# Placing edges in block-pair order: eight-tile groups that overlap, with counts made two groups ahead

## The reference, cut to what matters

```
h = relu(layernorm(x)); x = x + gated_conv(h, edge_attr, src, dst)   # z=[h[src],h[dst],e]; sigmoid(bn(zW1))*softplus(bn(zW2)), summed by dst
h = relu(layernorm(x)); x = x + sage(h, src, dst)                     # mean of h[src] by dst
h = relu(layernorm(x)); x = x + masked_hops(h, src, dst)              # three times: edge mask by a small MLP, then a sum by src
h = relu(layernorm(x)); x = x + edge_mlp(h, edge_attr, src, dst)      # mean over dst of MLP([h[src], e])
```

## Time and profile before

| what | value |
|---|---|
| time, median of three executions | 14558.93 us |
| the profiled execution: first to last instruction (span) | 14378.1 us |
| time outside the span (median less span) | 180.8 us |
| stage_place, from about 200 us to about 3440 us of the span | 3240 us |
| DVE busy over the whole span | 8318.0 us (58%) |
| PE busy over the whole span | 9017.0 us (63%) |
| POOL busy over the whole span | 4344.6 us (30%) |

### The profile page before, as it was taken

How to read it: one execution, slowest core, us unless ns; L and a number is a source line. 1 busy time by engine, 2 the same in 40 slices (tenths; PEclk the granted TensorE clock), 3 DMA queues, 4 the chain that set the end, 5 groups by cost and what they waited for, 6 DMA issues and landing times. The chain is left out here.

```text
span 14378.1 us, 449799 instructions
## 1 busy us (share of the span) xinstructions
PE 9017.0 (63%) x157729; PEld 8352.6 (58%) x157730; DVE 8318.0 (58%) x17981; ACT 6707.3 (47%) x18063; POOL 4344.6 (30%) x4481
## 2 busy tenths in 40 slices
PE   6444444444886555897777656666556765566776
PEld 6444444444886544887666556666556665566665
DVE  5333333334888999998163494552954619636146
ACT  0111111112897555896612425985248862389420
POOL 2444444443332000111151241431423414224044
PEclk9997555555998887998867868658676586775875
DMA  4222222101998776996974878869788697787886
GB/s 158 74 74 71 76 74 68 22 17 49 346 346 272 201 202 175 306 323 201 336 249 148 310 247 286 281 204 327 246 270 295 200 336 246 252 312 234 329 305 198
DMA packets 1161871, 3115.28 MB, mean 217 GB/s; under 512 B 367968, under 2 KB 652642, under 8 KB 1150562
## 3 DMA queue, kind: packets, MB, share of 16 engines
q1 hardware_dynamic: 899278, 2289.91, 45.4%
q0 software_dynamic: 262144, 823.09, 19.7%
q10 hardware_dynamic: 276, 0.01, 0.0%
HBM read 1917.81 MB, written 1128.54 MB: 212 GB/s over the span
## 5 line engine op out<-in xcount | busy, mean ns | idle before, releaser
L502 POOL DMA_INDIRECT rows_s<-place_rec,place_index x1568 | 1525.2, 973 | 1892.7 <-DVEq L623 1223.8
L2029 ACT ACTIVATE hop_parts<-hop_x,mask 128x64 f32<-128x64 f32 x6048 | 1524.3, 334 | 11.4 <-issue 7.0
L513 ACT COPY place_oh_turned<-place_turn_ps 100x1024 bf16<-100x1024 bf16 x197 | 199.4, 1012 | 2846.9 <-remote 2017.4
L1876 POOL DMA_INDIRECT mask_cols<-cols_all,mask_index x864 | 841.9, 974 | 2110.2 <-ACT mask_index L1883 1915.9
L2069 PE MATMUL hop_sums_ps<-hop_parts,hop_onehot 128*128 128x64 bf16 x18144 | 1123.9, 241 | 457.6 <-DVE hop_parts L2048 360.9
L2069 PEld LDWEIGHTS hop_sums_ps<-hop_parts,hop_onehot 128*128 128x128 bf16 x18144 | 988.5, 130 | 595.3 <-issue 594.9
L2013 POOL DMA_INDIRECT hop_x<-cols_all,hop_index x864 | 822.6, 952 | 1655.8 <-ACT hop_index L2020 988.0
L538 PE MATMUL place_same_ps<-place_oh_turned 100*128 100x128 bf16 x1568 | 197.5, 306 | 1652.5 <-ACT place_ohd_turned L514 1154.2
L2045 DVE TENSOR_TENSOR hop_parts<-hop_parts 128x448 f32<-128x448 f32 x864 | 540.4, 625 | 1198.4 <-ACT hop_parts L2029 1037.8
L538 PEld LDWEIGHTS place_same_ps<-place_oh_turned 100*128 100x128 bf16 x1568 | 151.3, 138 | 1670.5 <-issue 1670.5
L1959 DVE TENSOR_TENSOR mask_hidden<-mask_part_ps,mask_cols 128x448 f32<-128x448 f32 x864 | 534.4, 619 | 890.4 <-DMA mask_cols<-cols_all,mask_index 567.8
(11 more groups left out here) (382 smaller groups left out, 27979.1 us busy)
## 6 DMA issues: line engine op xcount, KB each, us to landing
cols_all<-att_in_rows SPq DMA_DIRECT2D x216, 896.0 KB
mask_onehot<-hot_s SPq DMA_DIRECT2D x216, 896.0 KB
cols_all<-hop_in_rows SPq DMA_DIRECT2D x216, 896.0 KB
hop_onehot<-hot_s SPq DMA_DIRECT2D x216, 896.0 KB
rows_all<-blank SPq DMA_DIRECT2D x72, 1808.0 KB
ct_u<-rows_all SPq DMA_DIRECT2D x288, 452.0 KB
cm_v<-rows_all SPq DMA_DIRECT2D x288, 448.0 KB, 3.7
cm_onehot<-hot_d POOLq DMA_DIRECT2D x288, 448.0 KB
```

Of the source, the lines that this page charges most:

```text
L502: nc.gpsimd.indirect_dma_start(m.rows_s.rearrange("p n w -> (p n) w"), bass.IndirectOffsetOnAxis(index[:, j, t:t + 1], 0), rec[:, j, t, :] ...
L1876: nc.gpsimd.indirect_dma_start(cols[:, s * 4 + i, :], None, table, bass.IndirectOffsetOnAxis(index[:, s * 4 + i, :], 0)).then_inc(arrived[ ...
L2029: last = nc.scalar.activation(parts[:, i, 0, t * F:(t + 1) * F], x[:, s * 4 + i, t, :], ACT.Copy, scale=mask[:, bass.ds(it * BATCH + t, 1)])
```

## The change

The diff touches `stage_place` and the size of `m.blk` (padding of 24 in place of 8 columns, since one-hots are now made three groups ahead). `turn_ps`, `run_ps` and `runs` get two buffers, `oh` four. The column `run_ps[:, 0, :]`, written once with zeros, makes the base counts of all eight tiles and the new total one operation (`start_runs`), and the total is kept in `runs[:, b, G, :]` in place of `m.run`. ACT signals `turned` after each of its two copies. PE's `find` is split into `compare` and `find`. PE's order becomes `count(g + 2)`, `compare(g + 1)`, `find(g + 1)`, in a loop over four groups per round, and DVE's `step(g)` makes the base counts of group g + 1, ranks group g, picks, makes the one-hots of group g + 3, and sums up. POOL's and SP's programs are unchanged.

```diff
--- before.py
+++ after.py
@@ -382,7 +382,7 @@
             @block.vector
             def _(dve):
                 o = Order(dve, order)
-                o.mark(nc.vector.memset(m.blk[:, EC:EC + 8, :], -1.0))
+                o.mark(nc.vector.memset(m.blk[:, EC:EC + 24, :], -1.0))
@@ -455,18 +455,19 @@
             return ctx.enter_context(nc.sbuf_tensor(f"place_{n}", s, d))
         rec = sb("rec", [P, 2, 16, RW])
         index = sb("index", [P, 2, 16], i32)
-        oh = sb("oh", [P, 2, G, 2, NBK], bf16)
+        oh = sb("oh", [P, 4, G, 2, NBK], bf16)
         oh_turned = sb("oh_turned", [2 * NBK, 2, G, P], bf16)
         ohd_turned = sb("ohd_turned", [NBK, 2, G, P])
-        runs = sb("runs", [NBK, G, 2 * NBK])
+        runs = sb("runs", [NBK, 2, G + 1, 2 * NBK])
         same = sb("same", [P, G, P], bf16)
         rank, slot = sb("rank", [P, 16]), sb("slot", [P, 16, 2])
         picked_v = sb("picked_v", [P, G, 2, NBK])
         ints = [sb(f"int{i}", [P, 16], i32) for i in range(8)]
         seventh = sb("seventh", [P, 16])
         we_parts = sb("we_parts", [P, 3, 3 * F], bf16)
-        turn_ps = ctx.enter_context(nc.psum_tensor("place_turn_ps", [P, G, P], bf16))
-        run_ps = ctx.enter_context(nc.psum_tensor("place_run_ps", [P, G + 1, NBK], fp32))
+        turn_ps = [ctx.enter_context(nc.psum_tensor(f"place_turn_ps{j}", [P, G, P], bf16)) for j in range(2)]
+        run_ps = [ctx.enter_context(nc.psum_tensor(f"place_run_ps{j}", [P, 512], fp32))[0:NBK, 0:(G + 1) * NBK]
+                  .rearrange("p (t n) -> p t n", n=NBK) for j in range(2)]
         same_ps = ctx.enter_context(nc.psum_tensor("place_same_ps", [P, G, P], fp32))
         slot_ps = ctx.enter_context(nc.psum_tensor("place_slot_ps", [P, G, P], fp32))
         e_came = [sem(f"e_came{j}") for j in range(2)]
@@ -507,48 +508,64 @@
 
             @block.scalar
             def _(act):
-                def turn_out(g, h):
+                def turn_out(g, b):
                     act.wait_ge(counted, g + 1)
+                    act.wait_ge(found, g)
                     act.sem_inc(gate, 1)
-                    nc.scalar.copy(oh_turned[:, h, :, :], turn_ps[0:2 * NBK, :, :])
-                    nc.scalar.copy(ohd_turned[:, h, :, :], turn_ps[0:NBK, :, :]).then_inc(turned, 1)
-                turn_out(0, 0)
+                    nc.scalar.copy(oh_turned[:, b, :, :], turn_ps[b][0:2 * NBK, :, :]).then_inc(turned, 1)
+                    nc.scalar.copy(ohd_turned[:, b, :, :], turn_ps[b][0:NBK, :, :]).then_inc(turned, 1)
+                act.sem_inc(found, 1)
+                act.wait_ge(counted, 1)
+                nc.scalar.copy(oh_turned[:, 0, :, :], turn_ps[0][0:2 * NBK, :, :]).then_inc(turned, 1)
+                nc.scalar.copy(ohd_turned[:, 0, :, :], turn_ps[0][0:NBK, :, :]).then_inc(turned, 1)
+                turn_out(1, 1)
                 with act.Fori(0, GROUPS // 2) as k:
                     for h in range(2):
-                        act.wait_ge(found, k * 2 + h + 1)
-                        turn_out(k * 2 + h + 1, 1 - h)
+                        turn_out(k * 2 + h + 2, h)
 
             @block.tensor
             def _(pe):
-                def count(g, h):
+                def count(g, h, b):
                     pe.wait_ge(hot, g + 1)
+                    pe.sem_inc(gate, 1)
                     for t in range(G):
-                        nc.tensor.transpose(turn_ps[0:2 * NBK, t, :], oh[:, h, t, :, :].rearrange("p i n -> p (i n)"), m.ident_b[:])
+                        nc.tensor.transpose(turn_ps[b][0:2 * NBK, t, :], oh[:, h, t, :, :].rearrange("p i n -> p (i n)"), m.ident_b[:])
                     for upto in range(1, G + 1):
                         for t in range(upto):
-                            last = nc.tensor.matmul(run_ps[0:NBK, upto, :], oh[:, h, t, 0, :], oh[:, h, t, 1, :],
+                            last = nc.tensor.matmul(run_ps[b][:, upto, :], oh[:, h, t, 0, :], oh[:, h, t, 1, :],
                                                     start=t == 0, stop=t == upto - 1)
                     last.then_inc(counted, 1)
 
-                def find(g, h):
-                    pe.wait_ge(turned, g + 1)
+                def compare(g, b):
+                    pe.wait_ge(turned, g * 2 + 1)
                     pe.wait_ge(ranked, g + 1)
                     pe.sem_inc(gate, 1)
                     for t in range(G):
-                        last = nc.tensor.matmul(same_ps[:, t, :], oh_turned[:, h, t, :], oh_turned[:, h, t, :], start=True, stop=True)
+                        last = nc.tensor.matmul(same_ps[:, t, :], oh_turned[:, b, t, :], oh_turned[:, b, t, :], start=True, stop=True)
                     last.then_inc(same_done, 1)
+
+                def find(g, b):
+                    pe.wait_ge(turned, g * 2 + 2)
                     pe.wait_ge(ran, g + 1)
                     pe.wait_ge(picked, g + 1)
                     pe.sem_inc(gate, 1)
                     for t in range(G):
-                        last = nc.tensor.matmul(slot_ps[:, t, 0:2 * NBK], ohd_turned[:, h, t, :], runs[:, t, :], start=True, stop=True)
+                        last = nc.tensor.matmul(slot_ps[:, t, 0:2 * NBK], ohd_turned[:, b, t, :], runs[:, b, t, :], start=True, stop=True)
                     last.then_inc(found, 1)
-                count(0, 0)
-                with pe.Fori(0, GROUPS // 2) as k:
-                    for h in range(2):
-                        find(k * 2 + h, h)
-                        pe.wait_ge(turned, k * 2 + h + 1)
-                        count(k * 2 + h + 1, 1 - h)
+                for j in range(2):
+                    nc.tensor.matmul(run_ps[j][:, 0, :], m.zeros_b[:, 0:NBK], m.zeros_b[:, 0:NBK], start=True, stop=True)
+                count(0, 0, 0)
+                count(1, 1, 1)
+                compare(0, 0)
+                find(0, 0)
+                with pe.Fori(0, GROUPS // 4) as k:
+                    for i in range(4):
+                        g = k * 4 + i
+                        pe.wait_ge(turned, g * 2 + 2)
+                        pe.wait_ge(ran, g + 1)
+                        count(g + 2, (i + 2) % 4, i % 2)
+                        compare(g + 1, (i + 1) % 2)
+                        find(g + 1, (i + 1) % 2)
 
             @block.vector
             def _(dve):
@@ -556,45 +573,51 @@
                 dve.sem_inc(ranked, 1)
                 dve.sem_inc(picked, 1)
                 o.mark(nc.vector.memset(rec[:, :, :, EF + 3:RW], 0.0))
-                for t in range(G):
-                    o.mark(nc.vector.tensor_copy(runs[:, t, NBK:2 * NBK], m.shift_d[:]))
+                for b in range(2):
+                    o.mark(nc.vector.tensor_copy(runs[:, b, 0:G, NBK:2 * NBK], b2(m.shift_d[:], G)))
 
                 def hots(at, h):
                     nc.vector.tensor_tensor(oh[:, h, :, :, :].rearrange("p t i n -> p (t i) n"), b2(m.numbers[:], 2 * G),
                                             b3(m.blk[:, at, :].rearrange("p t i -> p (t i)"), NBK), ALU.is_equal).then_inc(hot, 1)
 
-                def rank_group(g, h, s):
-                    dve.wait_ge(counted, g + 1)
+                def start_runs(b, before):
+                    nc.vector.tensor_tensor(runs[:, b, :, 0:NBK], run_ps[b][:, 0:G + 1, :], b2(before, G + 1), ALU.add).then_inc(ran, 1)
+
+                def step(g, i, s):
+                    half = i % 2
+                    dve.wait_ge(counted, g + 2)
+                    dve.wait_ge(found, g + 1)
+                    dve.wait_ge(ran, g + 1)
                     dve.sem_inc(gate, 1)
-                    s.mark(nc.vector.tensor_copy(runs[:, 0, 0:NBK], m.run[:]))
-                    s.then(nc.vector.tensor_tensor(runs[:, 1:G, 0:NBK], run_ps[0:NBK, 1:G, :], b2(m.run[:], G - 1), ALU.add))
-                    dve.sem_inc(gate, 1)
-                    nc.vector.tensor_tensor(m.run[:], m.run[:], run_ps[0:NBK, G, :], ALU.add).then_inc(ran, 1)
-                    hots(bass.ds(g * G + G, G), 1 - h)
+                    start_runs((i + 1) % 2, runs[:, half, G, 0:NBK])
                     dve.wait_ge(same_done, g + 1)
                     dve.sem_inc(gate, 1)
                     for t in range(G):
                         last = nc.vector.scalar_tensor_tensor(out=same[:, t, :], in0=same_ps[:, t, :], scalar=2.0, in1=m.after[:],
                                                               op0=ALU.is_equal, op1=ALU.mult,
-                                                              accum_out=rank[:, h * G + t:h * G + t + 1])
+                                                              accum_out=rank[:, half * G + t:half * G + t + 1])
                     last.then_inc(ranked, 1)
-                    dve.wait_ge(found, g + 1)
-                    dve.wait_ge(ran, g + 1)
+                    dve.wait_ge(found, g + 2)
+                    s.wait()
                     dve.sem_inc(gate, 1)
                     nc.vector.tensor_tensor(picked_v[:], slot_ps[:, :, 0:2 * NBK].rearrange("p t (i n) -> p t i n", i=2),
```

(14 more changed lines are left out.)

4 lines of the change are left out of this document (2 added, 2 removed).

## The result

On the chip that ran both, the kernel before took 14562.22 us (14557.95 to 14574.15) and the changed kernel **14138.85 us** (14123.64 to 14160.53), four runs each: ratio 0.971, interval 0.9698 to 0.9722. That is 423 us less. The forecast was 540 less and 14,019 us; it has the sign and most of the size, and the time lies in the range.

A forecast was written before the change was run, and what follows sets the result against it. The placing stage was taken as a chain of waits, 33.06 us a pair. Held signal at 20.3 plus 7.2 us gives 27.5, saving 545 us over 98 pairs; with +5 once, 14558.93 - 540 = 14,019 us, range 13,340 to 14,440.

The forecast's parts named there:

- The hold: In the placing stage, PE's signal from inside a POOL DMA burst arrives late: 12.9 us a pair, 95 times in 98.
- The end of the hold: Late signal comes 20.3 us after the burst begins (7.4 + 12.9), as before the change; at most +22.8 us.
- rival B: PE itself is held, so compare and find follow the hold: 31.4 us a pair, 14,400 us; chance 0.10.
- rival A: No hold left, POOL bounds the stage: 20.9 to 21.3 us a pair, 13,370 to 13,410 us; chance 0.25.
- The sentence on what would make it wrong altogether: Wrong if the hold grew with PE's instructions in a burst, or if time outside the stage moved; no size given.
- Main case: All the hold stays, 7.2 us of work follows: 27.5 us a pair, 14,019 us; DVE waits at picking; chance 0.47.
- second variant: The coming group's count is held at +5.8 us; DVE waits at base counts, 9.0 us follows in place of 6.2.
- Base counts: One DVE addition on 50x450, 0.61 us, replaces three operations: saves 0.28 us a group, 0.56 a pair.
- One-hots later: DVE's one-hots move behind the picking, ahead of `placed` for the second group: +0.99 us on that chain.
- C: The hold comes once per round of PE's loop: 24.2 us a pair on the mean, 13,690 us; chance 0.04.
- D: Slower: hold catches PE inside the count ahead of compare and find, 33.9 to 36.7 us a pair; chance 0.07.
- F: PE's longer loop body stalls on instruction fetch, 12.9 us in each of 49 rounds: 14,650 us; chance 0.02.

The follow-up runs named there:

- e3: Changed kernel with only the first of each pair's 16 indirect DMAs, stage alone read: 13.62 us a pair.
- e4: Changed kernel with a 512-column POOL memset (0.54 us) as a pause behind each indirect DMA: 13882.27 us, ratio to before 0.9662.
- e7: Kernel before with a 512-column POOL memset (0.54 us) as a pause behind each indirect DMA: 13838.67 us, ratio to before 0.9531.
- e9: Changed kernel with 8 count matmuls a group in place of 36 and a 304-column pause (0.37 us) behind each DMA: 13607.44 us, ratio to before 0.948.
- e10: Kernel before with 8 count matmuls a group in place of 36 and a 304-column pause (0.37 us) behind each DMA: 13542.19 us, ratio to before 0.9433.
- e12: Kernel before with only the first of each pair's 16 indirect DMAs, stage alone read: 19.56 us a pair.
- e2: Kernel before with 8 count matmuls a group in place of 36, nothing else: 13968.8 us, ratio to before 0.9719.
- e8: Kernel before with base counts and new total by one addition in place of a copy and two additions: 14341.88 us, ratio to before 0.9874.
- e11: Changed kernel with each DMA row writing 16 bytes in place of 144, to another table, stage alone read: 29.33 us a pair against 30.24.
- e1: Changed kernel with 8 count matmuls a group in place of 36: 13897.44 us, ratio to before 0.9671.
- e5: Changed kernel with 8 count matmuls a group in place of 36 and a pause giving DMAs 1.40 us apart: 13809.25 us, ratio to before 0.9504.

## Why the prediction was right, and where it was not

*The stage and the order of reading.* Right: the stage is a chain of waits, the rest is constant to 25 us, no more than other traces differ in it, and the gain is that of the waits that the new order takes out. The forecast of 540 us was 117 too high.

*The hold.* Half right. "PE's signal from inside a burst arrives late" is what happens: 97 late counts before, 55 after, none in the six kernels without a back-to-back burst (e3, e4, e7, e9, e10, e12). But the text made it a fixed delay that ends 20.3 us after the burst begins and leaves PE itself alone. Two terms failed:

- *The end of the hold.* Put at +20.3 (range to +22.8). In after the late signals come at +24.8 us (median), 4.8 us behind the end of POOL's last DMA. Before, the median is +21.4, and 46 of the 97 come while POOL is still writing, so they aren't tied to the burst's end.
- *PE's rate.* "PE has made the first group's find and the count after it" by +4.7 us, "at about +7.5 us PE ends L544 of the second group": PE's busy time of 15.0 us a pair was laid under the burst at full speed. From +12 us of a first burst to the end of the second PE begins 1 to 3 instructions per us, so the rest of the chain goes one instruction at a time until POOL stops. That is rival B's mechanism ("PE itself is held"), which was put at 0.10 because the matmuls 0.7 us apart in the earlier trace rows had been seen once.

*The sum.* 27.5 us a pair was forecast and 30.24 is in the trace; the ratio gives 423 / 98 = 4.3 us a pair gained against 5.56. It isn't one pair of 30 but a short one of 21 (rival A's value) and a long one of 38 to 41: counts two groups ahead let one burst start on the heels of the other, and then 32 DMAs pass with PE at a crawl. A steady 27.5 was wrong in kind, and that it is near the mean of 21 and 39.5 is partly luck. The base it was taken from was off as well: 33.06 is a trace of before with a span of 14378.1 us, and beside after before took 14,562.

*The sentence on what would make it wrong altogether.* Its first half came true: the loss grows with PE's instructions in a burst. e2 shows it: 28 matmuls and their loads less a group, 2.8% off the old order with no wait moved. The gain stood nevertheless, because the new order removes 5.9 us a pair of its own (19.56 to 13.62 without bursts), of which 4.3 are left with them.

*Where DVE's long wait is.* Main case: at the picking; second variant: at the base counts. It is at the base counts (L584, 1421.8 us, 45 waits; L603 has 67.8 us). So it is the count of the coming group that is held, for which the text had 9.0 us of tail: 20.3 + 9.0 = 29.3 us a pair, against 30.24. The choice of 7.2 between 6.2 and 9.0 is one step of the overestimate.

*Base counts.* One addition on 50x450 at 614 ns, forecast 0.61. The saving of 0.56 us a pair was right as DVE's time and too small for what e8 gained, 1.84 us.

*One-hots later.* L563's work follows the picking as said, at the same price (978 against 992 ns), and costs nothing that shows where the bursts bound:

```profile
L580 DVE TENSOR_TENSOR place_oh<-numbers,blk 128x800 bf16<-128x800 bf16 x196 | 191.7, 978 | 0.0
L584 DVE TENSOR_TENSOR place_runs<-place_run_ps,place_runs 50x450 f32<-50x450 f32 x196 | 120.3, 614 | 1542.2 <-remote 1421.8 <-issue 62.6 <-PE place_slot_ps L553 35.0
L503 POOL DMA_INDIRECT rows_s<-place_rec,place_index x1568 | 1554.4, 991 | 1586.0 <-DVEq L646 914.7 <-issue 671.3
```

The price appears in POOL's rows: 991 ns a DMA against 973, 16 x 18 ns = 0.3 us a pair, as the prediction had it (0.38). DMAs that begin beside one-hots took 1.34, 1.75, 1.92 and 2.11 us in place of 0.96. Nothing else of DVE's does this: with no one-hots beside them, the 1343 DMAs of before and all but the first of 1433 in after took at most 0.98 us, pickings, sums and rankings beside them included. A DMA that begins while one-hots run ends about 0.85 us after them (1517.86 against 1517.01 in e8's rows above), as if it had begun when they ended; one that is 0.4 us under way is not touched. The rule of the Trainium skill that the prediction weighed (SBUF — State Buffer, Who interferes with whom) agrees, since the one-hots are DVE's only long operation with both inputs in SBUF. The last bullet there, "PE and ACT never wait on anyone", stands among rules on SBUF's ports, and doesn't tell a reader what happens to PE here, whatever the cause.

*The rivals.* A's bound of 20.9 was met by every second pair only, and by the whole stage not even without late signals, since it takes a pause to be rid of them. C (once a loop round) had the right picture, one held pair and one free, and the wrong cause: e4's pause ends it without touching PE's loop. D's mechanism did occur: in the timeline above the slow stretch catches PE inside L535, ahead of L544 and L553. Those pairs, at 38 to 41 us, are even longer than its 33.9 to 36.7, but only every second pair is one of them, and the short ones outweigh them. F didn't occur, though the reason given against it was weak: a window of two pages of 256 instructions still holds today's body of some 280 recorded ones, so before's trace couldn't test it. After's can: in 300 to 3100 us the queues are those of the earlier trace rows, with no packets of instructions, so no fetch of the longer body is seen:

```profile
q1 hardware_dynamic: 201744, 150.28, 16.5%
q0 software_dynamic: 47291, 27.33, 4.1%
```

*Time outside the stage.* The prediction carried 180.8 us as a constant. It cancels in the difference, so it did the forecast no harm, but it was no time outside the span.

**What stays open.** Why PE slows and its signals come late while POOL writes descriptors back to back. The runs narrow it: it isn't the clock, not the bytes but for 0.9 us a pair at most (e11), not the order or one line of the code (both orders, counting, comparing and finding), not the presence of the DMAs (e4 has all of them, 0.4 us further apart); it grows with PE's instructions (e2). It is over within 5.2 us after the last DMA, and where PE has little to do often before it (46 of 97 late signals before, 56 of 97 in e8). A guess that fits, and that no run shows: something that both engines share falls behind and then has to catch up. All executions here were recorded by the profiler, so whether the records themselves are what is backed up was not told apart from semaphores or instruction supply. The Trainium skill (NOTIFIC — the notification-queue block, Overflow: three behaviours, one of which stalls the engine) says that the internal path of the event records holds its producers back rather than lose a record; no run here shows whether that is what PE meets. It matters for use: if it is the recording, a kernel that isn't profiled may have neither the loss nor the gain.

## What to carry to other kernels

When engines idle during a run of POOL's indirect DMAs, look at the intervals between PE's instructions before reordering the work: with PE slowed inside the burst, more work ahead fills the burst only in part. Try two cheap edits first, a pause of about 0.4 us behind each DMA and fewer, wider matmuls; here they brought 5.7% where the reordering brought 2.9%, and with them the reordering cost 65 us. (The reordering alone was timed only on the slowest chip; the two traces, 14378.1 against 14126.3 us, differ by 1.8%.) And compare two kernels by runs of one chip: this kernel's time moves by 1.4% from chip to chip (14,359 to 14,562), half the size of the effect looked for.

## What the runs showed of the hardware that was not expected

- POOL's indirect DMAs of 128 rows, begun every 1.26 us, leave PE 1 to 3 instructions per us after 12 us of a first burst (16 us in e1, where it has fewer to begin) and about 1 per us in a burst that follows at once, where it begins 17 per us at 1539.4 to 1556.3 us (147 matmuls and 147 loads in 16.9 us). The intervals in the crawl are near multiples of 0.7 us.
- At 1.68 us from start to start (e4, e7) there is none of it; at 1.40 us much of it is left (74 and 84 late counts); at 1.50 us with 158 instructions a pair none (e9, e10).
- PE's signals from a burst reach ACT and DVE 12.7 us late on the mean before and 26.8 after, and up to 5.2 us behind POOL's last DMA.
- The 36 count matmuls, each 50 columns wide, take 1.76 us at a granted clock of 0.50 (after) and of 1.00 (e12) alike.
- An indirect DMA that begins while DVE's one-hots run, two inputs in SBUF, ends about 0.85 us after them, up to 2.11 us in place of 0.96.
- Giving POOL 8.6 us more work a pair made the old order 4.7% faster.
- Before differs between chips by 203 us. Beside e4 and e7 it differs by 155, while e4 and e7 differ by 44 us where their periods (27.80 and 27.11) give 68, so by 24 us from chip to chip. What follows the stage takes 10,927 to 10,934 us in the traces of e4's chip (e1, e2, e4) and 10,932 to 10,953 in those of e7's (e5 to e8), 14 us apart on the mean. So most of the 155 us lies in the stage and goes with the bursts: probably it is held time, though there is no trace of before on the slower chip to show it.
